# Four waits between the first loads, the low part of the next context between pairs of weight sums, output weight sums behind the normalisation

## The reference

```
x = x + xattn(layernorm(x), ctx)           # 8 x 112 x 1024, ctx 8 x 375 x 1024
  q = x @ Wq                               # 32 heads of 128
  k, v = concat(ctx, x) @ Wk, @ Wv         # 4 key/value heads of 128, 487 keys
  out = softmax(q k / sqrt(128)) v @ Wo
x = x + ffn(layernorm(x))
  shared = relu(x @ up)**2 @ down          # 1024 -> 2048 -> 1024
  routed = (x @ fc1 @ expert) * sum(top2(x @ gate)) @ fc2
  layernorm(shared + routed) * gamma + beta
```

## Time and profile before

| | us |
|---|---|
| median of 3 runs | 1752.73 |
| range of the runs | 1751.73 to 1754.63 |
| the profiled execution | 1752.77 |
| its span | 1751.0 |
| TensorE busy | 1727.8 (99%) |
| VectorE, ScalarE, GpSimd busy | 962.9, 692.2, 961.4 |
| DMA | 296.31 MB, mean 169 GB/s |

### The profile page before, as it was taken

One profiled execution on the slowest core, in us unless ns is written; L12 is line 12 of the kernel. 1 busy time (PEld: TensorE's weight loads), 2 busy tenths in 40 slices (PEclk: granted clock), 3 DMA queues, 4 the chain that ended last, 5 costly groups with the idle time before them and its releaser, 6 DMA issues.

```text
span 1751.0 us, 24837 instructions
## 1 busy us (share of the span) xinstructions
PE 1727.8 (99%) x8613; PEld 1517.8 (87%) x8613; DVE 962.9 (55%) x1495; ACT 692.2 (40%) x1350; POOL 961.4 (55%) x785
## 2 busy tenths in 40 slices
PE   9999999999999999999999999999999999999997
PEld 8888998889999988988988898889888988888886
DVE  3521112634434357875887677767656364555567
ACT  3221112234343357733773477347512223332330
POOL 2546452235555548874767576736534245565557
PEclk9999999999999999999999999999999999999999
DMA  9888886256768658844773476334222212111223
GB/s 285 264 281 277 273 283 220 85 165 208 234 201 268 216 196 295 284 138 133 246 226 120 146 248 209 120 101 148 89 73 90 79 36 67 55 61 49 68 97 136
DMA packets 196567, 296.31 MB, mean 169 GB/s; under 512 B 19216, under 2 KB 158736, under 8 KB 195600
## 3 DMA queue, kind: packets, MB, share of 16 engines
q1 hardware_dynamic: 196496, 295.41, 51.5%
HBM read 197.10 MB, written 98.27 MB: 169 GB/s over the span
## 4 chain that ended last, share of the span: by engine, by line
PE 89%; DMA 4%; POOL 2%; DVE 2%; issue 1%; ACT 1%; SPq 1%; POOLq 0%; DVEq 0%; ACTq 0%
PE bank L1970 28%; PE bank L1971 28%; PE bank L1972 28%; PE bank L2187 5%; DMA tile_region<-in_ctxT 1%; DMA k_ctx_scratch<-small_region 1%; DMA slab_raw<-in_wkv 1%; DMA weight_sums_scratch<-slab_raw 1%; DMA slab_raw<-in_slabs 0%; DMA mid_region<-k_latents_scratch 0%; DMA small_region_unrounded<-in_slabs 0%; PE bank L2309 0%; PE bank L2013 0%; PE bank L2042 0%; POOL slab_raw L1034 0%
## 5 line engine op out<-in xcount | busy, mean ns | idle before, releaser
L951 POOL TENSOR_TENSOR tile_region<-tile_region,small 128x487 f32<-128x487 f32 x224 | 220.9, 1023 | 70.7 <-DVE small L1593 70.4
L1970 PE MATMUL bank<-mid_region 128*128 128x488 f32 (+4 forms) x532 | 219.1, 412 | 0.9 <-DVE mid_region L1648 0.5
L1972 PE MATMUL bank<-mid_region 128*128 128x488 f32 (+4 forms) x532 | 199.5, 375 | 0.0
L1971 PE MATMUL bank<-mid_region 128*128 128x488 f32 (+4 forms) x496 | 185.8, 375 | 0.0
L1970 PE MATMUL bank<-mid_region,act_region 128*125 128x512 f32 (+3 forms) x448 | 174.8, 390 | 0.8 <-POOL mid_region L1046 0.7
L1972 PE MATMUL bank<-mid_region,act_region 128*125 128x512 f32 (+3 forms) x448 | 174.3, 389 | 0.0
L1225 ACT ACTIVATE tile_region<-bank,small 128x487 f32<-128x487 f32 x224 | 153.5, 686 | 29.8 <-DVE small L1597 29.8
L1971 PE MATMUL bank<-mid_region,act_region 128*125 128x512 f32 (+3 forms) x418 | 162.7, 389 | 0.0
L935 POOL TENSOR_TENSOR slab_split<-slab_raw,slab_split 128x512 fp32r<-128x512 f32 x64 | 87.3, 1367 | 130.4 <-ACT slab_split L1180 130.4
L1257 ACT ACTIVATE mid_region<-bank 125x512 fp32r<-125x512 f32 x224 | 136.5, 612 | 56.1 <-PE bank L2187 56.1
L1597 DVE TENSOR_REDUCE small<-bank 128x1 f32<-128x487 f32 x224 | 145.7, 652 | 22.8 <-PE bank L1972 22.8
(11 more groups left out here) (243 smaller groups left out, 4332.7 us busy)
## 6 DMA issues: line engine op xcount, KB each, us to landing
slab_raw<-in_slabs SPq DMA_DIRECT2D x112, 256.0 KB, 3.6
q_scratch<-y_region SPq DMA_DIRECT2D x16, 1792.0 KB, 8.1
mid_region<-q_scratch SPq DMA_DIRECT2D x32, 896.0 KB, 6.8
slab_raw<-in_slabs SPq DMA_DIRECT2D x37, 512.0 KB, 3.4
weight_sums_scratch<-slab_raw SPq DMA_DIRECT2D x32, 512.0 KB, 5.2
v_scratch<-slab_split SPq DMA_DIRECT2D x8, 1536.0 KB, 8.1
slab_raw<-weight_sums_scratch SPq DMA_DIRECT2D x48, 256.0 KB, 4.5
mid_region<-v_scratch SPq DMA_DIRECT2D x32, 384.0 KB, 3.2
```

What stands on the lines that cost most here:

```text
L951: pool.tensor_tensor(PR[i][:, 0:KEYS], PR[i][:, 0:KEYS], rrow[:, i:i + 1].broadcast_to([P, KEYS]), ALU.mult).then_inc(s_pn, 1)
L1970: pe.matmul(out_ap, w[0], a[0], start=first, stop=False)
L1971: pe.matmul(out_ap, w[0], a[1], start=False, stop=False)
L1972: return pe.matmul(out_ap, w[1], a[0], start=False, stop=last)
```

## The change

Three hunks. The first adds waits on SyncE: piece 1 and piece 2 of the weights are issued only when the first or the second half of piece 0 has landed, and the context tiles beside them only when the first or the second tile has. The second changes the order on GpSimd: the low part of context b+1 stands ahead of the sums of pair 2b-1 instead of behind them. The third moves, for the first key/value head, the output sums of i = 3 to 6 behind the normalisation of their step, where those of i = 0 to 2 stood already.

```diff
--- before.py
+++ after.py
@@ -607,8 +607,11 @@
                 if k == 3:
                     sp.dma_start(CRAW[:, 2 * k:2 * k + 2, :], ctxT[0, :, 2 * k:2 * k + 2, :]).then_inc(s_first[k], 16)
                     sp.wait_ge(s_plo, 2)
+                else:
+                    sp.wait_ge(s_half[k - 1], 16)
                 sp.dma_start(PRAW[k % 3], wkv[k]).then_inc(s_piece[k % 3], 16)
                 if k < 3:
+                    sp.wait_ge(s_fhalf[k - 1], 16)
                     sp.dma_start(CRAW[:, 2 * k:2 * k + 2, :], ctxT[0, :, 2 * k:2 * k + 2, :]).then_inc(s_first[k], 16)
             for k in range(4, NK):
                 sp.wait_ge(s_plo, k - 1)
@@ -920,14 +923,13 @@
 
             ctx_lo(1, 1)
             pair_sums(0)
-            pair_sums(1)
             with pool.Fori(0, B // 2 - 1) as i:
                 for j in range(2):
                     ctx_lo(2 * i + j + 2, j)
+                    pair_sums(4 * i + 2 * j + 1)
                     pair_sums(4 * i + 2 * j + 2)
-                    pair_sums(4 * i + 2 * j + 3)
-            pair_sums(PAIRS - 2)
-            pair_sums(PAIRS - 1)
+            for j in range(PAIRS - 3, PAIRS):
+                pair_sums(j)
 
             def weight_blocks_lo(j):
                 for n in range(N_Q):
@@ -983,7 +985,7 @@
                 n = kv * B + 1
                 for j in range(B):
                     i = j if kv == 0 else j + 1
-                    late = kv == 0 and i < 3
+                    late = kv == 0 and i < B - 1
                     if 0 < j and i < B and not late:
                         output_sums(kv, i % 2, i // 2)
                     if j < B - 1:
```

## The result

| | before | after |
|---|---|---|
| median, us | 1753.57 (6 runs) | 1765.60 (6 runs) |
| range, us | 1750.38 to 1754.63 | 1760.75 to 1767.03 |
| profiled execution, us | 1752.77 | 1765.21 |
| its span, us | 1751.0 | 1763.4 |

The ratio is 1.0066, 95% interval 1.0053 to 1.0078: the change costs about 12 us. In a later session, beside the experiments, the same kernel took 1760.73 us against 1752.08 us, a ratio of 1.0050 (1.0037 to 1.0064), about 9 us. So the loss is real and lies between some 9 and 12 us.

A forecast was written before the change was run, and what follows sets the result against it. TensorE was taken as the bound, busy 1727.8 of 1751.0 us, with a side chain almost as long. Terms 0 + 19.1 - 1.1 = +18.0 us on 1752.8 us gave 1770.8 us, range 1766 to 1775 us (8 in 10: 1761 to 1776).

The forecast's parts named there:

- Step one and two: Contexts 2 and 3: the 1.24 us wait at context 2 goes; the chain is 2.8, then 9.2 us late.
- Step three: Rounds for pairs 5, 7, 9, 11: each loses 2.7 us, so pair 11's first store is 20.0 us late.
- Step four: Latent transposes: second wait 12 to 13 us; sixth start at 286.0 us, and everything from there is 19.1 us late.
- 0.9 us of slack: Sixth latent transposes: their gate opened at about 265.97 us, 0.9 us before their start at 266.87 us.
- The load of context 5: SyncE, context stage: if issued before 150 us, the lag doesn't build up and the forecast is wrong.
- The two waits of over 15 us together: TensorE before its second and sixth latent transposes: two waits, together over 15 us, as a sign of being right.
- Part 1: First loads: 0.8 us gain at TensorE that doesn't reach the end; 0 in the sum, -1 to +1 us.
- Part 3: Attention near 696 us: the 1.08 us wait goes, -1.1 us; price taken as 0, at most 1.1 us.
- The context copy: Context loads: landing in about half of 9.27 us, the chain keeps TensorE's pace; 1754.5 us, chance 0.07.
- The side chain: Context stage: rival that the side chain isn't the bound and three waits go; 1749.6 us, chance 0.09.
- the rival of a smaller loss: Context stage: only step two is smaller, or a few rounds lose less; 1758 to 1765 us, chance 0.12.
- The clock rival: TensorE after the long transpose waits: lower clock level returns, costing up to 3 us at the end; 1773.8 us, chance 0.17.

The follow-up runs named there:

- the dose of eight memsets: Kernel before plus eight memsets of an idle buffer on GpSimd ahead of the sums of pair 13; 1754.57 us, ratio 1.0019.
- part 1 alone: Kernel before with only the first hunk, the added SyncE waits in the first loads; 1752.80 us, ratio 1.0002.
- 16 memsets: Kernel before plus 16 memsets of an idle buffer on GpSimd ahead of the sums of pair 13; 1769.23 us against 1752.08 us, ratio 1.0096.
- part 2 alone: Kernel before with only the second hunk, GpSimd's low parts ahead of the odd pairs' sums; 1759.87 us, ratio 1.0046.
- the kernel with K1 first: Changed kernel with the store of K1 ahead of the odd pair's stores on SyncE; 1751.67 us against 1751.20 us of before, ratio 1.0000.

## Why the prediction was right and where it was off

**Direction and place: right.** Slower, by waits at the second and sixth latent transposes, released by VectorE behind ScalarE's K evictions, behind stores that SyncE issues late. The fifth waited too, for 0.90 us, which the forecast didn't name.

**Step one and two: right within a microsecond.** The low part of context 2 followed at once, and the wait of 1.24 us at context 2 went. The forecast put the store of pair 3 9.2 us late; it was 10.2 us late. Of that, 1.2 us is a later start: ScalarE's high part of context 2 was at 58.30 us instead of 57.09 us. Executions differ by that much: the load of context 1 landed at 32.19 us in this trace, at 29.74 us in the later trace of the same kernel, and between 27.00 and 32.19 us over all traces.

**Step three, the cost of a round: the term that was mis-sized.** The forecast was 2.7 us a round, 10.8 us in four. From the store of pair 3 to that of pair 11 the changed kernel took 241.34 - 108.36 = 132.98 us, before took 226.28 - 98.18 = 128.10 us: 1.2 us a round, 4.9 us in four. Two links were shorter than the rows of before had them. A context landed 8.99, 7.98, 8.74 and 8.09 us after its issue (for example 121.11 to 130.10 us), 8.45 us on average instead of the 9.27 us of the earlier trace rows. And the leg from the odd pair's store to the next load of a context took 12.6 us on average (142.30 to 154.61 us is 12.3 us), where before took 13.3 us: I had called it the same. The links of a chain were added up at the prices that they had beside other traffic. Once the work is serial, there is less traffic beside each link. The traces agree in part: over the loads of contexts 4 and 5 the DMA engines were 95 and 96% busy, at 305 and 309 GB/s, before; over those of contexts 4 to 7 they were 84 to 95% busy, at 266 to 299 GB/s, in the changed kernel. That this is the reason is still an inference; what is shown is that both links were shorter.

**Step four: right in kind, with two corrections.** From the store of pair 11 to the eviction of K3 of context 7 the changed kernel took 277.16 - 241.34 = 35.8 us against 38.1 us before, so the lag shrank again, from 15.1 us to 12.7 us; the forecast held it constant. Less 0.9 us of slack this is 11.8 us, and the sixth transposes were 12.0 us late. The sum of the profiled executions is 1752.8 + 12.0 = 1764.8 us before part 3, the measured one 1765.2 us. The slack was right for the execution that it was read from, but it isn't a property of the kernel: the dose of eight memsets found 6.7 us. The forecast took it from a trace whose side chain ran late, so it took nearly the smallest slack and with it the largest loss; in the first session the changed kernel's chain ran late too. That the first median fell inside the range of 1761 to 1776 us is in part luck: the same kernel's 1760.73 us is outside it.

**Signs.** The load of context 5 was issued at 154.61 us, behind the 150 us that would have spoken against the chain. The two waits of over 15 us together didn't come: it was three waits of 9.6 us together. The ends were added up a little wide as well: 1770.8 + 1 + 1.1 + 1.2 = 1774.1 us, not 1775.

**Part 1: the price at TensorE was wrong, its weight right.** The forecast gave TensorE 0.8 us there. The wait grew from 1.27 to 2.27 us in the changed kernel, partly because TensorE had finished the first tiles sooner, and its products of piece 1 started 0.3 us later. It didn't reach the end in any way that can be measured, as forecast: part 1 alone is no measurable change.

**Part 3: the wait went, the gain did not arrive.** The forecast took the price at 0 of a range of 0 to 1.1 us. It was about half: 0.5 us more waiting for VectorE in the output products. In the changed kernel that wait is 0.9 us, and the waits for the loads of k rose from 0.4 to 0.9 us, so the 1.1 us is gone almost entirely.

**The rivals.** The context copy came sooner than 9.3 us but far from 4.6 us, and the chain kept growing. The side chain was the bound. What came is in kind the rival of a smaller loss (1758 to 1765 us, chance 0.12), in which a few rounds lose less: the first session lies 0.6 us above it, the later one inside. The clock rival was half right: the lower level came back after the 7.38 us wait, as the last section shows, but its cost was hidden in the later waits, and after these, of 0.90 and 1.32 us, the clock stayed up. The Trainium skill (TensorE: Matmul & The Clock Gate, HAM oscillation) says that waits send TensorE back to the throttled clock; the changed kernel's trace agrees for the wait of 7.38 us, with a granted clock of 0.64 behind it.

## What to carry to other kernels

When a producer's work is moved ahead of another's on one queue, ask who waits for the work that is put back, and follow it through every in-order queue to an eviction: here a shift of 2.8 us on GpSimd grew over five contexts to 15 us, where a store that frees a buffer stood behind a wait that had nothing to do with it, and only to 3.0 us where it stood ahead. A busy share of 99% doesn't say how far the side chains are from becoming the bound, and the slack read in one execution can be several microseconds off. Moving the one freeing store ahead of the unrelated wait removed the whole loss.

## What the runs showed of the hardware

**The clock after a wait.** Windows of the changed kernel (us, then busy us and counts of PE, PEld, DVE, ACT and POOL, the granted clock, DMA share, GB/s):

```profile
12.00:15.00 3.00, 2.73 (x10) 2.77 (x11) 2.19 (x3) 1.64 (x3) 0.00 (x0) 0.62 0.96 297
250.00:256.00 6.00, 0.80 (x5) 0.83 (x5) 3.36 (x6) 2.87 (x6) 4.67 (x8) 0.64 0.85 271
256.00:262.00 6.00, 6.00 (x31) 5.97 (x31) 0.62 (x1) 1.02 (x3) 1.12 (x2) 0.79 0.73 244
262.00:268.00 6.00, 6.00 (x38) 5.97 (x38) 1.08 (x2) 0.44 (x2) 5.24 (x8) 1.00 1.01 392
```

The granted clock was 0.62 of full in the stretch after the 2.27 us wait of the first loads, and 0.64 and 0.79 after the 7.38 us wait, so TensorE ran at the lower of its two levels for part of each. From the second to the third transposes it took 261.26 - 255.20 = 6.06 us, the next took 4.53 us: 1.5 us lost. With 16 memsets, behind a wait of 12.86 us, the stretch was all at the lower level:

```profile
274.00:280.00 6.00, 0.54 (x3) 0.57 (x4) 1.68 (x3) 1.41 (x3) 4.09 (x6) 0.50 0.83 238
```

There the leg from the sixth to the seventh transposes took 288.20 - 279.46 = 8.74 us, where before has 272.83 - 266.87 = 5.96 us: 2.8 us lost, and nothing behind hides it. In the other traces the waits of 3.84 and 5.24 us (part 1 alone, part 2 alone) were followed by a granted clock of 0.55 (79 to 82 us) and 0.59 (250 to 256 us). At the first loads a wait of 2.44 us in the kernel with K1 first and one of 2.02 us in the later trace of the changed kernel left it at 1.00, where the one of 2.27 us did not. So for these short waits the length alone doesn't say which comes.

**VectorE beside a long GpSimd instruction.** A scaling of 112 x 1024 elements on VectorE took 4.47 us at 71.92 us of the trace of before, while GpSimd's low part of context 2 ran, and 0.81 us at 62.01 us. In the kernel with K1 first it took 4.50 us at 60.78 us beside the same low part, and no time was lost by it at the end. Why it takes longer was not examined.

**A second pace of the query stage.** In the profiled execution with eight memsets the rounds of the query stage, from one store of queries to the next, took 17.36 us each behind the first one, in all other traces some 17.02 us. From the first of 14 such stores to the last it took 224.9 us, where before took 220.3 us. These 4.5 us arise far from the place of the edit, and they are the larger part of why that execution took 1758.8 us with 1.37 us of added waiting. Single runs of before reach 1758.95 us as well. What sets the pace was not examined and stays open.
